# Pairwise products of a recommendation tower: half of the passes take eight fields, and VectorE sums the others

## The reference

```python
e = jnp.stack([tbl_0[ids[:, 0]], ..., tbl_31[ids[:, 31]]], axis=1)   # 1024 x 32 x 64
p, q = e[:, ROW], e[:, COL]                  # 496 pairs (i < j) of the 32 fields
kp = jnp.einsum('bpj,ipj->bpi', p, kernel)   # kernel: 64 x 496 x 64
z = jnp.sum(kp * q, axis=-1)                 # 1024 x 496
h = jnp.concatenate([z, dense_ctx], axis=1)  # 1024 x 512
h = jnp.maximum(h @ W_top1 + b_top1, 0.0)    # 512 x 512
h = jnp.maximum(h @ W_top2 + b_top2, 0.0)    # 512 x 256
y = h @ W_top3                               # 1024 x 1
```

## Time and profile before

| | us |
|---|---|
| median of 3 runs | 412.73 (412.15 to 414.6) |
| the profiled execution | 412.47 |
| its span | 410.7 |
| TensorE (PE) busy | 403.8 |
| VectorE (DVE) busy | 301.9 |
| ScalarE (ACT) busy | 252.1 |
| GpSimd (POOL) busy | 231.7 |

### The profile page before, as it was taken

One profiled execution on the slowest core, in us unless ns is written; L12 is line 12 of the kernel. 1 busy time (PEld: TensorE's weight loads), 2 busy tenths in 40 slices (PEclk: granted clock), 3 DMA queues, 4 the chain that ended last, 5 costly groups with the idle time before them and its releaser, 6 DMA issues.

```text
span 410.7 us, 10179 instructions
## 1 busy us (share of the span) xinstructions
PE 403.8 (98%) x3421; PEld 253.5 (62%) x3421; DVE 301.9 (74%) x305; ACT 252.1 (61%) x1862; POOL 231.7 (56%) x251
## 2 busy tenths in 40 slices
PE   7899999999999999999999999999999999999997
PEld 4566666576675656676666666676666666654442
DVE  6968878878787887878879797869879788740000
ACT  3158877766677867665696867619978568002111
POOL 6777777777777757776776776677767200000000
DMA  6667661121371102111311113011311020000000
GB/s 178 188 195 212 211 181 28 37 67 30 75 184 27 29 19 69 37 28 27 76 31 25 28 26 79 21 27 28 79 25 29 12 51 2 2 2 0 2 0 1
DMA packets 18266, 24.31 MB, mean 59 GB/s; under 512 B 6387, under 2 KB 11767, under 8 KB 17958
## 3 DMA queue, kind: packets, MB, share of 16 engines
q1 hardware_dynamic: 10406, 15.64, 13.1%
q0 software_dynamic: 7808, 8.01, 9.7%
HBM read 19.44 MB, written 0.00 MB: 47 GB/s over the span
## 4 chain that ended last, share of the span: by engine, by line
PE 93%; POOL 3%; DMA 2%; issue 1%; ACT 0%
PE u_ps L666 41%; PE z_ps L700 14%; PE u_ps L687 13%; PE z_ps L706 7%; PE u_ps L747 7%; PE t_ps L623 4%; PE u_ps L767 3%; POOL nat L416 3%; PE u_ps L673 2%; DMA nat<-tbl,ids_sb 2%; DMA ids_sb<-ids 1%; PE t_ps L653 0%; PE u_ps L775 0%; ACT y_sb L552 0%
## 5 line engine op out<-in xcount | busy, mean ns | idle before, releaser
L416 POOL DMA_INDIRECT nat<-tbl,ids_sb x244 | 230.5, 945 | 88.9 <-issue 56.8
L586 DVE TENSOR_TENSOR prod<-u_ps,rows 128x1024 f32<-128x1024 f32 x184 | 213.2, 1216 | 53.2 <-PE u_ps L666 53.2
L501 ACT ACTIVATE pass_prod<-pass_prod 128x64 f32<-128x64 f32 x896 | 214.3, 243 | 22.1 <-DVE pass_prod L597 22.1
L666 PE MATMUL u_ps<-rows,k_sb 64*128 64x256 f32 x1472 | 174.9, 384 | 0.0
L501 ACT ACTIVATION_READ_ACCUMULATOR pass_prod<-pass_prod 128x1 f32 x896 | 170.0, 190 | 0.0
L666 PEld LDWEIGHTS u_ps<-rows,k_sb 64*128 64x128 f32 x1472 | 137.8, 187 | 45.9 <-DVE pass_prod L597 13.4
L597 DVE TENSOR_TENSOR pass_prod<-u_ps,nat 128x1024 f32<-128x1024 f32 x56 | 67.1, 1212 | 0.0
L687 PE MATMUL u_ps<-k_sb,rows 64*128 64x256 f32 x448 | 61.6, 394 | 0.6 <-ACT rows L489 0.6
L700 PE MATMUL z_ps<-prod,sel 128*32 128x512 f32 x512 | 61.6, 598 | 0.0
L489 ACT ACTIVATE rows<-t_ps 128x512 f32<-128x512 f32 (+1 forms) x38 | 19.6, 515 | 56.5 <-PE t_ps L623 51.5
L687 PEld LDWEIGHTS u_ps<-k_sb,rows 64*128 64x128 f32 x448 | 40.5, 186 | 14.9 <-DVE prod L586 10.0
(11 more groups left out here) (44 smaller groups left out, 76.9 us busy)
## 6 DMA issues: line engine op xcount, KB each, us to landing
by_self<-rows SPq DMA_DIRECT2D x32, 128.0 KB
nat<-tbl,ids_sb POOLq DMA_INDIRECT x244
k_sb<-kern SPq DMA_DIRECT2D x3, 768.0 KB, 6.2
k_sb<-kern SPq DMA_DIRECT2D x2, 640.0 KB, 3.8
k_sb<-kern SPq DMA_DIRECT2D x1, 1152.0 KB, 5.6
k_sb<-kern SPq DMA_DIRECT2D x2, 512.0 KB, 3.6
rows<-w SPq DMA_DIRECT2D x1, 1024.0 KB, 6.5
rows<-tbl SPq DMA_DIRECT2D x4, 224.0 KB
```

What stands on the lines that cost most here:

```text
L416: pool.indirect_dma_start(nat_of(m, n)[:, h * EMBED:(h + 1) * EMBED], None, tables[f], bass.IndirectOffsetOnAxis(ids_sb[:, col:col + 1], 0 ...
L501: op = nc.scalar.activation(of, of, ACT.Copy, accum_out=z_nat[:, b % 2, s, row:row + 1])
L586: nc.vector.tensor_tensor(to, u, by.unsqueeze(1).to_broadcast([P, 2, 2, SIZE]), ALU.mult).then_inc(prod_ready, 1)
L666: op = nc.tensor.matmul(u[:, h, :], k_sb[part, k_of(d), side, :], rows[part, tile, cols_of(b)], start=True, stop=True)
```

## The change

Tiles 6 to 13 (`WIDE`) no longer share passes. Each has **wide passes** of its own against eight fields, 0 to 7: two 512-column matmuls for each half (L768 in the code of after), multiplied with four tiles of natural rows (`nat03`, L659), summed by ScalarE as before (L552), with half of the sums going to a new `z_wide`. The other tiles (2, 3, 4, 5, 14, 15) keep passes of four fields, but VectorE sums them, with one reduction of 128x1024 to 128x16 right behind the product (L665). Per block that makes 6 narrow and 16 wide passes, 22 in all, and 40 doubles (20 quads) in place of 48 (24). `z_wide` is added to `z_ps` by eight small matmuls at the last quad of a block, and that quad waits for the block's wide sums. In block 0, where tiles 2 and 3 exist in `rows` only, `turn_back` transposes them back, and ScalarE copies them to `nat03`. The ring of other natural tiles shrinks from 8 to 5, the planner deals out sums at 5 or 7 per piece, and the first-layer weights are arranged to match.

```diff
-IN_PASSES = [((tile, 0), (tile, 1)) for tile in range(2, TILES)]
+WIDE = (6, 7, 8, 9, 10, 11, 12, 13)
+IN_PASSES = [((tile, 0), (tile, 1)) for tile in range(2, TILES)] + [((tile, 2), (tile, 3)) for tile in WIDE]
...
-NP = len(IN_PASSES) // 2 * SUBS
+PASSES = [(tile,) if tile in WIDE else (tile, tile + 1) for tile in range(2, TILES) if tile in WIDE or tile % 2 == 0]
+NP = len(PASSES) * SUBS
...
-URING, PRING, CRING, RING, LANES = 3, 8, 3, 8, 8
+def by_scalar(j):
+    return pass_of(j)[0][0] in WIDE
...
+URING, PRING, CRING, RING, LANES = 3, 8, 3, 5, 8
 BURST = 4
+
+RATE = (5, 7)
...
-        self.add_sums(6 if len(self.open) == CRING or self.doubles >= (BLOCKS - 1) * ND else 4, 2)
+        self.add_sums(RATE[len(self.open) == CRING or self.doubles >= (BLOCKS - 1) * ND], 2)
...
-                if m >= LANES:
-                    pool.wait_ge(transposed, m - LANES + 1)
+                if tiles_in_front(m):
+                    pool.wait_ge(transposed, tiles_in_front(m))
...
                 if first == 0:
                     act.wait_ge(prod_ready, AT[b, None, j] + 1)
+                    if b > 0 and tiles == WIDE[0:1] and s == 0:
+
+                        act.wait_ge(summed, b * QUADS)
...
+                if n == BACK_AT:
+                    act.wait_ge(turned_back, 1)
+                    nc.scalar.activation(nat03[:, 0, :, 2:4, :].rearrange("p s t c -> p t s c"), t_ps[:], ACT.Copy).then_inc(nat_ready, 1)
...
-                if k >= CRING:
-                    dve.wait_ge(pass_summed, k - CRING + 1)
-                by = nat01[:, b % 2, pass_of(j)[1]].rearrange("p t n -> p (t n)").unsqueeze(1).unsqueeze(1)
+                if k >= CRING and by_scalar((k - CRING) % NP):
+                    dve.wait_ge(pass_summed, wide_passes(k - CRING + 1))
+                tiles, s = pass_of(j)
+                if tiles[0] in WIDE:
+                    if b == 0:
+                        dve.wait_ge(nat_ready, 1)
+                    by = nat03[:, b % 2, s].rearrange("p (x t) n -> p x (t n)", x=2).unsqueeze(1)
+                else:
+                    by = nat03[:, b % 2, s, 0:2].rearrange("p t n -> p (t n)").unsqueeze(1).unsqueeze(1)
                 nc.vector.tensor_tensor(pass_prod[:, k % CRING], u, by.to_broadcast([P, 2, 2, SIZE]), ALU.mult).then_inc(prod_ready, 1)
+                if not by_scalar(j):
+                    row = pass_row(tiles[0], 0, 0)
+                    if b >= 2:
+                        dve.wait_ge(z_transposed, b - 1)
+                    dve.wait_ge(prod_ready, n + 1)
+                    nc.vector.tensor_reduce(z_nat[:, b % 2, s, row:row + SUMS], pass_prod[:, k % CRING].rearrange("p h t (f n) -> p (h t f) n", f=4),
+                                            mybir.AxisListType.X, ALU.add).then_inc(pass_reduced, 1)
...
+                if turned:
+                    pe.wait_ge(nat_ready, 1)
...
+            def turn_back(tiles):
+
+                pe.wait_ge(rows_ready, tiles)
+                for t in range(2):
+                    for s in range(SUBS):
+                        op = nc.tensor.transpose(t_ps[:, t, s, :], rows[:, 2 + t, s * P:(s + 1) * P], ident[:])
+                op.then_inc(turned_back, 1)
...
+                        if tile in WIDE:
+                            op = nc.tensor.matmul(u_ps[:, n % URING, h].rearrange("p x n -> p (x n)"), rows[part, tile, at:at + P],
+                                                  k_sb[part, k:k + 2].rearrange("p d s n -> p (d s n)"), start=True, stop=True)
...
+                    if last:
+
+                        pe.wait_ge(pass_summed, (b + 1) * NW)
+                        for s in range(SUBS):
+                            for k in range(4):
+                                op = nc.tensor.matmul(z_ps[32 * k:32 * k + 32, 0, s * P:(s + 1) * P], z_wide[:, s, 32 * k:32 * k + 32], ident[:],
+                                                      start=False, stop=s == SUBS - 1)
```

More of the change, by code:

```diff
@@ L69, in pass_of, with wide_passes @@
 def pass_of(j):
-    return 2 + 2 * (j // SUBS), j % SUBS
-URING, PRING, CRING, RING, LANES = 3, 8, 3, 8, 8
+    return PASSES[j // SUBS], j % SUBS
+def by_scalar(j):
+    return pass_of(j)[0][0] in WIDE
+def wide_passes(k):
+    return k // NP * NW + sum(by_scalar(j) for j in range(k % NP))
+URING, PRING, CRING, RING, LANES = 3, 8, 3, 5, 8
 BURST = 4
+RATE = (5, 7)
 def quads_behind(n):
@@ L123, in lane_count, with tiles_in_front @@
     return 32 * SUBS * (m // LANES + (m % LANES not in BY_PRODUCT))
+IN_TURN = [m for m in range(LOOKED_UP) if tile_at(m)[1] >= 4 and m not in BY_PRODUCT]
+def tiles_in_front(m):
+    place = IN_TURN.index(m) if m in IN_TURN else 0
+    return max(0, m - LANES + 1, IN_TURN[place - RING] + 1 if place >= RING else 0)
 AHEAD = 30
@@ L159, in __init__ @@
             self.add_sums(SUMS, 0)
+        if self.folds < BLOCKS:
+            self.folded[-1] = self.folds
+            self.folds += 1
     def landed(self, m):
@@ L269, in add_pass @@
         self.append((b, None, j))
-        self.open.append([len(self.order) - 1, b, j, 0])
+        if by_scalar(j):
+            self.open.append([len(self.order) - 1, b, j, 0])
+        elif j == NP - 1:
+            self.summed.append(len(self.order))
         self.passes += 1
@@ L558, in _ @@
             nc.vector.memset(z_nat[:], 0.0).then_inc(z_zero, 1)
+            nc.vector.memset(z_wide[:], 0.0).then_inc(wide_zero, 1)
             dve.wait_ge(one_line_ready, 1)
@@ L612, in fill, with transpose @@
                     nc.tensor.matmul(u_ps[:, n % URING, 0, 0, 0:P], ident[:], ident[:], start=True, stop=True)
-            def transpose(m, count, folds):
+            def transpose(m, count, folds, turned):
                 for t in range(m, m + count):
@@ L677, in interact_pass @@
             def interact_pass(n, b, j):
-                first, s = pass_of(j)
+                tiles, s = pass_of(j)
                 at = b * SIZE + s * P
@@ L722, in _ @@
                     else:
-                        transpose(m, count, folds)
+                        transpose(m, count, folds, n > BACK_AT)
                     tiles += count
-                needed = tile_of(d) if d is not None else pass_of(j)[0] + 1
+                needed = tile_of(d) if d is not None else pass_of(j)[0][-1]
                 while k_here < needed:
@@ L733, in _ @@
                 for m, count in PLAN.behind[n]:
-                    transpose(m, count, folds)
+                    transpose(m, count, folds, n > BACK_AT)
                     tiles += count
+                if n == BACK_AT:
+                    turn_back(tiles)
                 for quad in PLAN.quads[n]:
@@ L810 @@
                         w1_rows[z_row(DOUBLES.index(double), bank, half, side)] = w1_in[pair]
+                    elif s >= 2:
+                        w1_rows[2, wide_row(tile, bank, 2 * s + half)] = w1_in[pair]
                     else:
```

57 lines of the change are left out of this document (35 added, 22 removed).

## The result

The changed kernel takes 434.21 us (433.49 to 437.73, 4 runs) against 412.83 beside it: ratio 1.0513, 95% interval 1.048 to 1.0546. The profiled execution took 433.65 with a span of 431.6.

The account below looks back on a forecast made before the run. The prediction took VectorE's step of 1.14 us per piece, not TensorE's matmuls, as the bound. 412.5 - 6.4 (fewer additions) + 2.4 (z_wide) + 1.5 (turn back) + 15.5 (reductions) + 7 (copies) = 432.5 us, range 409 to 443.

Parts of the forecast that it names:

- the price list: Main stage priced by pieces, not matmuls: 1.14 us per piece, 0.80 per burst with its addition into z_ps.
- the reductions: 24 sums of narrow passes on VectorE, 1.25 us each, showing in clusters: +15.5 us of 30.
- fewer additions: Bursts per block, each with an addition into z_ps, go from 12 to 10: -6.4 us.
- z_wide: Eight 128-column matmuls at each block's last quad, 0.6 us per block: +2.4 us, bounds 1.6 and 3.5.
- turn back: Four transposes in block 0, waiting for ScalarE to empty t_ps: +1.5 us, bounds 0.6 and 1.9.
- T: A transpose pair on TensorE, priced as 0.59 us added to its burst.
- the hand calculation: Stretches around block boundaries followed by four rules from profile rows, giving what reductions and waits for copies would show.
- The copies: ScalarE's copies of t_ps to rows stand behind sums, so doubles wait: +7 us, between zero and 9.3.
- TensorE as the bound: Rival: TensorE's matmuls bound the kernel, so four fewer quads per block save 15.4 us: 401 us, chance 0.07.
- The swallowed reductions: Rival: VectorE's idle gaps swallow the reductions, so the change takes 410 us, chance 0.12.
- Copies free: Rival: ScalarE keeps up, so copies cost nothing: 425.5 us, chance 0.18.
- ScalarE as the bound: Rival: ScalarE's sums of wide passes hold VectorE through the pass_prod ring, 15 us over three blocks: 445 us, chance 0.07.

Follow-up runs that it names:

- e3: Changed kernel without the 24 reductions on VectorE and with ScalarE making only every fourth sum of a wide pass: 408.08 us, ratio 0.987.
- e1: Changed kernel with the 24 reductions on VectorE left out, all else the same: 415.12 us, ratio 1.0048.
- e4: Changed kernel with each of the 24 reductions on VectorE made twice, with a wait between: 467.56 us, ratio 1.1295.
- e7: Kernel before, with its 24 passes of tiles 2 to 5, 14 and 15 summed on VectorE: 492.32 us on the slow chip, 431.32 us again at usual pace.
- e2: Changed kernel with ScalarE making only every fourth of the 16 sums of a wide pass: 428.37 us, ratio 1.0358.
- e5: Changed kernel with passes in another order, narrow and wide alternating at a block's start: 502.87 us on the slow chip, 429.78 us again at usual pace.
- e6: Changed kernel with sums due just ahead of a transposed tile issued behind its copy on ScalarE: 501.87 us on the slow chip, 431.27 us again at usual pace.
- e9: Changed kernel with all 22 passes of a block summed by ScalarE, none by VectorE, 8 sums per piece: 524.56 us, ratio 1.076, slow chip only.

## Why the prediction was right

434.2 was measured for 432.5, and the mechanism held: pieces at VectorE's step, reductions that show in clusters, copies behind sums. The parts are less exact than the total. By e3, e1 and the changed kernel they are -5.1 + 7.0 + 19.3 = 21.2, where the forecast had -2.5 + 7 + 15.5 = 20.0: the price list came out 2.6 too dear and the reductions 3.8 too cheap, and that these two errors nearly cancel is luck.

- **The price list** (fewer additions -6.4, z_wide +2.4, turn back +1.5, together -2.5): e3 gives -5.1. z_wide is 0.55 per block [the end rows above], as said, and turning back 1.4 (in e3 TensorE goes from 27.24 to 28.67 with it). The list is 2.6 us too dear, and really by more, since e3 still has 4.2 us of waits for copies, which the list doesn't hold. One reason is in e3's trace: the list charges T at 0.59 wherever it stands, but in front of further pieces of a long burst TensorE waits for VectorE anyway. The burst of eleven pieces from 273.42 to 286.61 takes 13.19, where the list gives 11 x 1.14 + 0.80 + 0.59 = 13.93, and one of nine (191.49 to 202.41) 10.92 for 11.65. Bursts of six with T behind their last piece take 8.22, as listed. The two long bursts make 1.5 us of the miss; the rest I have not placed.
- **The reductions** (+15.5): 19.3 (e1), by the other way round 20.3. The mechanism was right, the size too small. Burst by burst, the changed kernel against e3, it is 3.8, 5.2 and 7.4 at the three block boundaries (forecast: 3.3, 3.3, 4.6), 2.4 at the start (2.6) and 1.5 at the end (1.7), 20.3 in all. One reduction costs 1.32 with its wait, not 1.25, at 24 of them 1.7 us at most. And TensorE's clock, which the sum left out, fell in the clusters of two boundaries: 0.6 of the 5.2 and 1.1 of the 7.4 (next section). Against e1 this makes only 1.0, since the clock fell once in e1 too, at a cost of 0.7. Some 1.4 us of the miss is left; there the gaps swallowed less than the hand calculation had. Doubling them (e4) shows what the prediction rested on, that VectorE's gaps are full near the clusters; e7 shows that it isn't a property of the new order alone.
- **The copies** (+7): 6.0 and 7.0 (e2, e1 against e3). The +7 was a choice between zero and the hand calculation, whose five terms add up to 9.8 and not to 9.3; by it the total would have been 3 us further up. The dearest was where the prediction put it, in block 1, where the first wide sum also waits for block 0's last addition. ScalarE's rows, then TensorE's:

```profile
127.41 0.26 ACT L552 ACTIVATE pass_prod<-pass_prod 128x64 f32<-128x64 f32 x1 [7.04 <-PE z_ps L797]
...
135.12 0.59 ACT L532 ACTIVATE rows<-t_ps 128x512 f32<-128x512 f32 x1
```

```profile
132.46 0.66 PE L694 MATMUL t_ps<-ident,nat 128*128 128x128 f32 x4
135.86 1.13 PE L746 MATMUL u_ps<-rows,k_sb 64*128 64x256 f32 x8 [2.74 <-ACT rows L532]
```

The first sum of the block waits 7.04 us for z_wide's addition, so the copy of tiles 8 and 9, behind 30 sums, starts at 135.12, 2 us after the transpose ended, and TensorE waits 2.74. In block 2 the hand calculation had 0.5 for this copy, and there was none; the later one at tile 10 cost the 0.84 that was said (0.9). Block 3 had 3.0 and shows 1.80, block 0 had 1.6 and shows 1.03 + 0.66. All waits of doubles:

```profile
PE u_ps L746 <- ACT rows L532: 7.9, 6, 2.7
```

- **The price of one reduction.** The Trainium skill, "VectorE: DVE Perf Modes", section "Rules for kernel authors", advises restructuring away from tensor_reduce on a hot path. The trace agrees: 1.220 us for 1024 elements per partition, and 19 us of end-to-end time for 29.3 us of it. The Trainium skill, "VectorE: DVE Perf Modes", section "The DRAIN you can't avoid", says, from a row of copies, that a semaphore between two operations costs nothing. The measurement here differs, and it decides: a product and the reduction that waits for it stand 0.10 apart and two reductions that wait for each other 0.03 (e4), while independent products overlap by 0.08. So the hand-over costs 0.18 or 0.11. No run has such a pair without the wait, so what of it is the semaphore stays open.
- **The rivals.** TensorE as the bound (401) is out by e3 and e1. The swallowed reductions (410) are out by e1 and e4. Copies free is out by e2. ScalarE as the bound is out by e2: with three of four sums of the wide passes gone, the time fell by 6.0 us and no more. The smaller ring of natural tiles (8 to 5) had been put at nothing, and the trace agrees: before, TensorE waited once for a gathered tile, 0.9 us, and in the changed kernel its waits list no gather.
- **The signs.** VectorE is busy 331.8 us (329 said), ScalarE 282.3 (283), and the first layer starts at 386.23 (385). One sign failed: TensorE was to stay above 95% busy, and it is 93%, since TensorE stands idle in the clusters and before copies.

## What to carry to other kernels

An engine that is 98% busy in the profile can still be paced by another: look at what the next piece of a burst costs, and compare it with the step of each neighbour. If another engine's step is that price, as VectorE's was here, then work added to it costs in full once its gap behind the burst is full, and the gap holds only what stands in that one burst. Before work is moved from one engine's queue to another's, see which small hand-over (here a copy) stands behind the work that was added.

## What the runs showed of the hardware

TensorE's granted clock, 1.00 throughout in the profiled execution of before, fell where clusters of reductions left TensorE idle. Windows of after: TensorE's busy time and, in the third number from the right, its clock, in a plain stretch, in the cluster of four narrow passes, and just behind.

```profile
219.00:235.00 16.00, 15.16 (x120) 8.57 (x120) 14.28 (x13) 14.67 (x114) 11.31 (x12) 1.00 0.15 28
296.00:306.00 10.00, 6.25 (x31) 3.10 (x29) 9.59 (x9) 0.60 (x1) 4.17 (x5) 0.80 0.27 69
306.00:310.00 4.00, 4.00 (x52) 1.95 (x50) 3.90 (x4) 0.04 (x1) 0.88 (x1) 0.66 0.05 8
```

Behind the gaps shown above, of at most 1.32 us each, the clock fell from 2.4 to 1.2 GHz: 0.80 and 0.66 are averages over windows with both levels in them, and from 304 to 308 it was 0.50. The Q at 306.38 took 3.07 us for 1.93, and another at 215.38 took 2.50. These two are the 1.7 us. In e4 TensorE was idle longer, and the clock was 0.949 on average (after 0.988, e1 0.996, e3 0.999). Reductions are not needed for it. In e1 it fell behind the gap of 2.74 us for a copy in block 1, and the Q at 132.01 took 2.66 for 1.92:

```profile
132.01 2.66 PE L776 MATMUL z_ps<-prod,sel 128*32 128x512 f32 x16
```

And two of the seven executions of the kernel before beside e5b had 0.996 and took 414.55 and 414.98 us, where the middle one took 412.93. The Trainium skill, "TensorE: Matmul & The Clock Gate", section "HAM oscillation — how this bites in real kernels", says that a TensorE whose bursts have idle stretches between them falls back to the lower clock, there with waits of 3 to 5 us for data. The trace agrees that it falls back, by the 0.80 and 0.66 above, but here gaps of at most 1.32 us went before it.

One chip, that of e5, e6, e7 and e9, ran everything at another pace: the kernel before took 488.96 us there. The instructions last as long as elsewhere (e7 there):

```profile
L601 DVE TENSOR_TENSOR prod<-u_ps,rows 128x1024 f32<-128x1024 f32 x184 | 214.2, 1218 | 72.5 <-PE u_ps L689 64.5 <-PE u_ps L710 6.2 <-remote 0.9
...
L618 DVE TENSOR_REDUCE z_nat<-pass_prod 128x16 f32<-128x1024 f32 x24 | 29.3, 1220 | 1.6
```

but hand-overs are late. A piece that TensorE began at 290.36 was multiplied from 293.60, 3.24 us later, where the way takes 1.18:

```profile
290.36 2.86 PE L689 MATMUL u_ps<-rows,k_sb 64*128 64x256 f32 x24
```

```profile
293.60 4.62 DVE L601 TENSOR_TENSOR prod<-u_ps,rows 128x1024 f32<-128x1024 f32 x4 [2.59 <-PE u_ps L689]
```

On that chip e7 cost 0.6%, and on another 4.3%. VectorE's gaps before its doubles are longer there, 72.5 us for 41.3 in e7b, so I read it that the reductions do fall into them; no run tests that reading. What makes hand-overs late there stays open.
